# Max products on four banks with maxima taken in pairs, and scores on one pair of banks, in a fused decoder layer

## The chip, the core and the metric

The kernel runs on one core of a Trainium2 chip. The engines of the core, PE (TensorE, matrix products into PSUM), DVE (VectorE), ACT (ScalarE), POOL (GpSimd) and SP (SyncE, which issues most of the DMAs), each run an instruction stream of their own and meet at semaphores. PSUM is used as eight banks of 128 x 512 f32, `ps[:, 0]` to `ps[:, 7]`. The metric is the time of one execution in microseconds (us), the median of the runs.

## The reference, cut to what matters

One decoder layer on four batch rows of 512 tokens. Each batch runs through an attention with 16 heads of 32, a state-space model (a scan over 512 steps for 16 states) and a gated feed-forward, each followed by a layer norm. What the change touches is the softmax of the attention:

```python
q, k, v = heads(x @ Wq), heads(x @ Wk), heads(x @ Wv)
scores = jnp.einsum('bhqd,bhkd->bhqk', q, k) / jnp.sqrt(jnp.float32(D))
attn = jax.nn.softmax(scores, axis=-1)
std = jnp.einsum('bhqk,bhkd->bhqd', attn, v)
```

A softmax needs the maximum of each row of scores before it takes exponentials. Beside it stands a second attention by affinities to eight "splats" of each head, blended in with a small weight.

## The kernel before, in words

The batches run one behind the other. In a batch the attention is computed in four groups j = 0 to 3 of four heads each (`NG` = 4, `HG` = 4). The scores are computed twice.

First, as max products: for each group 16 tiles (four heads by four query tiles, numbered n = 16 j + i in the batch), a matmul each (`max_scores`, L1303) of 128 queries by 512 keys into bank 0 or 1 in turn. DVE takes the maximum over the keys (`max_tiles`, L960) into a column of `MX`. PE may start tile n when DVE has reduced tile n - 2 (`s_mx`). When all 16 are there, PE transposes the maxima (`transpose_max`, L1309), ACT negates them (`bias_row`, L642) and sends them by a DMA into a row of `QS`, from where the second scores get them as an additional row of the product.

Second, as transposed scores with the maximum subtracted: in the loop of `attention_phase` on PE, for each group four steps kt = 0 to 3 over the key tiles, and in each step two pairs of heads p = 0, 1 (L1413). ACT takes the exponential of a pair, two banks at once, into `PT` (L731, `s_exp`). The pairs stand in banks 2, 3 and 4, 5; a pair of scores waits for the exponential of the pair before the last. Only in group 3 of all but the last batch both pairs use banks 4 and 5, since banks 2 and 3 serve the preparation of the next batch there. Then `values` (L1320) multiplies the exponentials with V into bank 6, and with ones into bank 7 for the denominators; it runs one step behind the scores. The first call of a group into bank 6 waits until `normalise` of the group before has read banks 6 and 7 (`s_nrm`, L967).

Around this, while group j is in its score loop, the max products of group j + 1 are put between its matmuls, and DVE takes their maxima: `X_CHUNK` says how many of the 16 tiles in which step (for j = 0 tiles 4 to 8, 8 to 14, 14 to 16; for j = 1 and 2 tiles 0 to 4, 4 to 10, 10 to 16 in steps 0, 1 and 2), and `cuts` how many behind which pair. The first four tiles of group 1 (`X_AHEAD`) run before the loop.

Each engine works in the order of its program. On DVE a step of the loop is: the maxima, `normalise` of the group before (L966 to L970; for j = 2, `KV_GROUP`, ahead of the maxima, together with `splat_kv`, L1010, which needs the KV product of L1420), for j = 0 in step 1 the splat work (L979 to L993), and then halves of the state-space scan (`scan_half`: L896, the scan itself L904, L907). In batch 0 three or four halves fall to a group, one in step 1 and the others in step 3; in the other batches two, in step 3. On ACT a step is: decay exponentials for the scan (L593), in step 3 the bias row, and the two exponentials; at the turn to the next group `inverse_start` (a logarithm, L661, and an exponential, L663) stands ahead, for j = 1 a copy too (L712), and for j = 0 four splat exponentials follow step 0 (L649, L650).

## Time and profile before

| | us |
|---|---|
| median of three runs | 1462.55 |
| lowest, highest run | 1458.94, 1462.65 |
| the profiled execution | 1458.29 |
| its span, first to last instruction | 1456.5 |
| PE, DVE, ACT busy in it | 1211.8, 1204.7, 764.0 |

The profile is of one execution. A row of the timeline gives start, duration, engine, line of the kernel, operation, tiles, the number of instructions merged into it, and in brackets how long the engine was idle ahead of it and what ended that. PE overlaps its matmuls, so that the durations of neighbouring rows overlap; the distance of two starts says more. PEclk is the granted clock of PE: 1.00 is 2.4 GHz, 0.50 is 1.2 GHz.

### The profile page before, as it was taken

Reading aid. Unit: us, or ns where it says so; the run is one execution under the profiler, and the core shown is the slowest. Engines: PE = TensorE matmul, PEld = TensorE weight load, DVE = VectorE, ACT = ScalarE, POOL = GpSimd, SP = SyncE. Lnnn points to the kernel's source line nnn. Section 1 sums busy time; section 2 is a strip of 40 time slices with the busy share of each in tenths; the row PEclk is TensorE's granted clock in tenths of the full one; section 3 lists DMA queues with packets and bytes.
Section 4 is the critical chain, followed back from the end, with each engine's and each line's share of the span. In section 5 each row is a group of like instructions: output and inputs, shape, how many; then the busy total and the mean of one; then the engine's idle time right before and its main releaser. Section 6 shows DMA issues by size and latency. Waiting matters only on the chain.

```text
span 1456.5 us, 14224 instructions
## 1 busy us (share of the span) xinstructions
PE 1211.8 (83%) x4698; PEld 558.9 (38%) x4698; DVE 1204.7 (83%) x1457; ACT 764.0 (52%) x1118; POOL 164.9 (11%) x211
## 2 busy tenths in 40 slices
PE   5563885788689989889899898889799898877996
PEld 3332422233245543333345533333355433323553
DVE  5878898989979998879889997889799998786223
ACT  6865543535367753537477653545677545352331
POOL 1000111001101120100101121001111211001001
PEclk8765796878979999789899997899799997788998
DMA  6853796465339959553259686362289595540231
GB/s 193 288 162 116 172 255 165 102 145 145 58 89 248 251 133 266 127 132 87 67 135 272 164 225 194 90 164 51 89 230 259 119 256 133 146 95 15 66 101 44
DMA packets 112666, 220.20 MB, mean 151 GB/s; under 512 B 14560, under 2 KB 25312, under 8 KB 112592
## 3 DMA queue, kind: packets, MB, share of 16 engines
q1 hardware_dynamic: 88608, 142.85, 31.9%
q0 software_dynamic: 18432, 67.12, 23.9%
q10 hardware_dynamic: 5552, 9.31, 1.8%
q8 instruction: 38, 0.62, 0.2%
q14 instruction: 36, 0.29, 0.1%
HBM read 122.37 MB, written 29.62 MB: 104 GB/s over the span
## 4 chain that ended last, share of the span: by engine, by line
PE 38%; DVE 38%; issue 9%; ACT 4%; DVEq 0%; ACTq 0%; POOL 0%; POOLq 0%
DVE ST L904 14%; PE ps L1381 6%; DVE ST L896 5%; PE ps L1514 5%; PE ps L1303 5%; DVE MX L960 5%; PE ps L1320 4%; PE ps L1458 3%; PE ps L1378 3%; PE ps L1474 3%; PE ps L1413 2%; DVE QAK L1131 2%; DVE QS L1118 2%; DVE ST L907 1%; PE ps L1286 1%
## 5 line engine op out<-in xcount | busy, mean ns | idle before, releaser
L904 DVE TENSOR_TENSOR_SCAN ST<-dA,ST 128x1024 f32<-128x1024 f32 x128 | 292.9, 2289 | 12.9 <-ACT dA L593 10.2
L1514 PE MATMUL ps<-V,GU 128*128 128x512 f16 x1024 | 238.0, 387 | 5.6 <-DVE V L1105 5.6
L960 DVE TENSOR_REDUCE MX<-ps 128x1 f32<-128x512 f32 x256 | 165.2, 686 | 72.8 <-PE ps L1303 72.3
L509 POOL DMA_DIRECT2D YA<-ST x128 | 109.3, 854 | 975.6 <-DVE ST L907 923.8
L593 ACT ACTIVATE dA<-DL,Aneg 128x511 f32<-128x511 f32 x256 | 168.3, 713 | 60.6 <-DVE ST L904 56.4
L731 ACT ACTIVATE PT<-ps 128x1024 f32<-128x1024 f32 x128 | 126.8, 1021 | 135.7 <-PE ps L1413 135.0
L1303 PE MATMUL ps<-KS,QS 96*128 96x512 f32 x256 | 127.4, 562 | 50.1 <-DVE MX L960 37.1
L907 DVE TENSOR_TENSOR ST<-ST,BC 128x1024 f32<-128x1024 f32 x128 | 156.8, 1225 | 4.4
L896 DVE TENSOR_TENSOR ST<-DU,BC 128x1024 f32<-128x1024 f32 x128 | 155.9, 1218 | 0.1
L1514 PEld LDWEIGHTS ps<-V,GU 128*128 128x128 bf16 x1024 | 97.0, 99 | 140.6 <-issue 30.5
L1474 PE MATMUL ps<-QS 128*128 128x512 f32 x512 | 142.9, 422 | 2.5 <-DVE QS L1118 1.6
L1381 PE MATMUL ps<-XA,W 128*128 128x512 f32 x256 | 113.3, 595 | 0.0
L1303 PEld LDWEIGHTS ps<-KS,QS 96*128 96x128 f32 x256 | 56.5, 235 | 145.2 <-DVE MX L960 99.4
L1474 PEld LDWEIGHTS ps<-QS 128*128 128x128 f32 x512 | 97.6, 194 | 34.9 <-DVE QS L1118 11.3
L1413 PE MATMUL ps<-QS,KS 97*128 97x512 f32 x256 | 100.2, 490 | 6.6 <-ACT PT L731 5.6
L1131 DVE TENSOR_TENSOR QAK<-QAK,ps 128x512 f32<-128x512 f32 x64 | 43.7, 683 | 62.3 <-PE ps L1514 62.3
L1320 PE MATMUL ps<-PT,V 128*32 128x512 f32 x512 | 82.3, 720 | 12.4 <-ACT PT L731 9.9
L782 ACT CAST QS<-QAK 128x512 fp32r<-128x512 f32 x64 | 39.6, 618 | 95.2 <-DVE QAK L1131 95.2
L1320 PE MATMUL ps<-PT,ones 128*32 128x512 f32 x512 | 74.2, 654 | 0.0
L1413 PEld LDWEIGHTS ps<-QS,KS 97*128 97x128 f32 x256 | 52.0, 222 | 54.2 <-issue 27.7
L1381 PEld LDWEIGHTS ps<-XA,W 128*128 128x128 f32 x256 | 48.0, 190 | 62.6 <-issue 62.2
L1378 PE MATMUL ps<-W,XA 128*128 128x512 f32 x128 | 61.3, 639 | 4.2 <-ACT V L676 3.4
(231 smaller groups left out, 1539.9 us busy)
## 6 DMA issues: line engine op xcount, KB each, us to landing
YA<-ST POOLq DMA_DIRECT2D x128, 512.0 KB, 7.2
BC<-bc_rows SPq DMA_DIRECT2D x64, 512.0 KB, 8.0
GU<-gu_tiles SPq DMA_DIRECT2D x64, 256.0 KB, 4.6
QS<-proj_tiles SPq DMA_DIRECT2D x64, 256.0 KB, 4.2
QS<-qk_parts SPq DMA_DIRECT2D x32, 256.0 KB, 4.1
KS<-qk_parts SPq DMA_DIRECT2D x32, 256.0 KB, 5.5
ST<-in_L_ffn_w_gate_up_dram SPq DMA_DIRECT2D x16, 256.0 KB, 3.7
gu_tiles<-BC SPq DMA_DIRECT2D x16, 256.0 KB, 2.1
```

What stands on the lines that cost most here:

```text
L593: last = nc.scalar.activation(dA[:, a, e, 1:S], DL[:, 2 * a + e, 1:S], ACT.Exp, scale=Aneg[:, 2 * a + e, n:n + 1])
L731: nc.scalar.activation(PT[:, kt % 2, 2 * p:2 * p + 2, :], ps[:, bank:bank + 2, :], ACT.Exp, scale=SCALE).then_inc(s_exp, 1)
L896: nc.vector.tensor_tensor(ST[:, ring(bb, n, a), :, :], DU[:, 2 * a:2 * a + 2, :], BC[:, n % BC_RING, 0:1, :].broadcast_to((P, 2, S)), ALU. ...
L904: nc.vector.tensor_tensor_scan(flat, dA[:, a, :, :].rearrange("p e s -> p (e s)"), flat, 0.0, ALU.mult, ALU.add).then_inc(s_scan, 1)
L907: nc.vector.tensor_tensor(st, st, BC[:, n % BC_RING, 1:2, :].broadcast_to((P, 2, S)), ALU.mult).then_inc(s_prod, 1)
L960: nc.vector.tensor_reduce(MX[:, j % 2, qt, h:h + 1], ps[:, n % 2, :], AX_X, ALU.max).then_inc(s_mx, 1)
L1303: mm(ps[:, n % 2, :], QS[i][0:3 * D, h, qt * P:(qt + 1) * P], KS[i][0:3 * D, h, :], start=True, stop=True).then_inc(s_xs, 1)
L1320: last = mm(ps[D * h:D * h + D, bank, :], w, PT[:, kt % 2, h, :], start=(kt == 0), stop=(kt == KT - 1), tile_position=(0, D * h))
L1381: last = mm(bank, W[:, z, k, j * P:(j + 1) * P], XA[:, k, :], start=(k == 0), stop=(k == KT - 1))
L1413: last = mm(ps[:, score_bank(b, j, h), :], KS[i][0:3 * D + 1, h, kt * P:(kt + 1) * P], QS[i][0:3 * D + 1, h, :], start=True, stop=True)
L1474: last = mm(ps[:, 4 + r, :], HL[:, 2 * z + t % 2, r * P:(r + 1) * P], WP[:, t % WP_RING, :], start=(t == 0 and z == 0), stop=(t == NT - 1 ...
L1514: last = mm(ps[:, f % F_RING, :], GU[:, t % GU_RING, k, m * P:(m + 1) * P], XHL[:, z, k, :], start=(k == 0 and z == 0), stop=(k == KT - 1 ...
```

## The change

From tile n = 20 on (`FIRST_MAX_PAIR`: the 16 tiles of group 0 and the first four of group 1 stay as they are) the max products go to banks 0 to 3 in turn, and DVE takes the maxima of two tiles in one reduction over two banks. PE may start a pair when DVE has reduced the pair before the last. For this the scores give banks 2 and 3 away: in every group and batch both pairs of heads use banks 4 and 5, and a pair waits for the exponential of the pair just before it. In groups 0 to 2 the two `values` calls of a step move from behind both score pairs and their first max products to places between: bank 6 behind the first pair, bank 7 behind the second, each ahead of the max products of that place.

```diff
-        def score_bank(b, j, h):
-
-            return 4 + h % 2 if j == NG - 1 and b + 1 < B else 2 + h
+        def score_bank(h):
+
+            return 4 + h % 2
+
+        def max_bank(n):
+
+            return n % 2 if n < FIRST_MAX_PAIR else n % 4
...
+        FIRST_MAX_PAIR = 4 * KT + X_AHEAD
...
             def max_tiles(b, j, lo, hi):
-                for i in range(lo, hi):
+                pairs = 16 * j + lo >= FIRST_MAX_PAIR
+                for i in range(lo, hi, 2 if pairs else 1):
                     n = 16 * j + i
                     h, qt = i // KT, i % KT
-                    dve.wait_ge(s_xs, 16 * NG * b + n + 1)
-                    nc.vector.tensor_reduce(MX[:, j % 2, qt, h:h + 1], ps[:, n % 2, :], AX_X, ALU.max).then_inc(s_mx, 1)
+                    bank = max_bank(n)
+                    if pairs:
+                        dve.wait_ge(s_xs, 16 * NG * b + n + 2)
+                        nc.vector.tensor_reduce(MX[:, j % 2, qt:qt + 2, h], ps[:, bank:bank + 2, :], AX_X, ALU.max).then_inc(s_mx, 2)
...
-                    if n >= 2:
+                    if n >= FIRST_MAX_PAIR + 2:
+                        pe.wait_ge(s_mx, 16 * NG * b + n // 2 * 2 - 2)
+                    elif n >= FIRST_MAX_PAIR:
+                        pe.wait_ge(s_mx, 16 * NG * b + FIRST_MAX_PAIR)
+                    elif n >= 2:
                         pe.wait_ge(s_mx, 16 * NG * b + n - 1)
...
                             s = 2 * (KT * j + kt) + p
-                            if s < 2:
+                            if s == 0:
                                 pe.wait_ge(s_dist, 2 * (b + 1))
                                 pe.wait_ge(s_pj2, 2 * (b + 1))
                             else:
-                                one_pair = j == NG - 1 and not last_batch
-                                pe.wait_ge(s_exp, 2 * KT * NG * b + (s if one_pair else s - 1))
+                                pe.wait_ge(s_exp, 2 * KT * NG * b + s)
...
+                            if j < NG - 1 and kt > 0:
+                                values(b, j, kt - 1, 6 + p)
                             max_scores(b, j + 1, cuts[p], cuts[p + 1])
...
                         for p in range(2):
-                            if kt > 0 and j < NG - 1:
-                                values(b, j, kt - 1, 6 + p)
                             max_scores(b, j + 1, cuts[2 + p], cuts[3 + p])
```

## Rows read from the trace of the kernel before

**Rows 1.** The page, part 1: busy time, share and instructions of each engine.
```profile
PE 1211.8 (83%) x4698; PEld 558.9 (38%) x4698; DVE 1204.7 (83%) x1457; ACT 764.0 (52%) x1118; POOL 164.9 (11%) x211
```
**Rows 2.** The page, part 4: the chain that ended last, by engine.
```profile
PE 38%; DVE 38%; issue 9%; ACT 4%; DVEq 0%; ACTq 0%; POOL 0%; POOLq 0%
```
**Rows 3.** Waits, 880 to 985 us: us in total, times, longest us.
```profile
DVE MX L960 <- PE ps L1303: 19.9, 22, 2.4
...
PE ps L1303 <- DVE MX L960: 5.3, 7, 1.7
```
**Rows 4.** Stretches: us, busy time (instructions) of PE, PEld, DVE, ACT, POOL, PEclk, DMA.
```profile
902.00:912.00 10.00, 9.91 (x26) 5.35 (x26) 5.72 (x10) 6.31 (x8) 2.27 (x3) 0.50 0.28 54
...
930.00:936.00 6.00, 5.07 (x14) 1.84 (x15) 4.23 (x7) 1.61 (x2) 0.00 (x0) 0.50 0.71 169
...
937.00:957.00 20.00, 16.89 (x89) 6.48 (x81) 17.50 (x20) 9.98 (x13) 1.70 (x2) 1.00 0.50 116
```
**Rows 5.** The page, part 5: groups; busy us, mean ns of one, idle ahead.
```profile
L960 DVE TENSOR_REDUCE MX<-ps 128x1 f32<-128x512 f32 x256 | 165.2, 686 | 72.8 <-PE ps L1303 72.3
...
L896 DVE TENSOR_TENSOR ST<-DU,BC 128x1024 f32<-128x1024 f32 x128 | 155.9, 1218 | 0.1
...
L1131 DVE TENSOR_TENSOR QAK<-QAK,ps 128x512 f32<-128x512 f32 x64 | 43.7, 683 | 62.3 <-PE ps L1514 62.3
```
**Rows 6.** Timeline of batch 2, j = 0, end of kt 1: start us, us.
```profile
909.27 1.94 PE L1320 MATMUL ps<-PT,V 128*32 128x512 f32 x8
...
911.14 1.22 PE L1303 MATMUL ps<-KS,QS 96*128 96x512 f32 x2
...
913.18 0.87 DVE L979 TENSOR_SCALAR X<-X,par 128x512 f32<-128x512 f32 x2
...
916.59 1.28 DVE L960 TENSOR_REDUCE MX<-ps 128x1 f32<-128x512 f32 x2
```
**Rows 7.** Timeline of batch 2, j = 0 kt 3 and j = 1 kt 0.
```profile
919.98 1.94 ACT L731 ACTIVATE PT<-ps 128x1024 f32<-128x1024 f32 x2 [0.71 <-PE ps L1413]
...
921.97 1.06 PE L1320 MATMUL ps<-PT,V 128*32 128x512 f32 x8 [0.67 <-ACT PT L731]
...
924.24 1.18 PE L1413 MATMUL ps<-QS,KS 97*128 97x512 f32 x4
...
925.60 1.94 ACT L731 ACTIVATE PT<-ps 128x1024 f32<-128x1024 f32 x2
...
927.23 2.57 DVE L960 TENSOR_REDUCE MX<-ps 128x1 f32<-128x512 f32 x4
...
927.96 1.10 PE L1303 MATMUL ps<-KS,QS 96*128 96x512 f32 x2 [1.66 <-DVE MX L960]
```
**Rows 8.** Timeline of batch 2, j = 1, kt 0 to kt 2.
```profile
930.31 0.74 DVE L967 SCALAR_TENSOR_TENSOR X<-ps,par,RD 128x512 f32<-128x512 f32 x1
...
933.75 1.94 PE L1320 MATMUL ps<-PT,V 128*32 128x512 f32 x8
...
937.74 0.73 PE L1413 MATMUL ps<-QS,KS 97*128 97x512 f32 x2
...
938.31 0.63 PE L1303 MATMUL ps<-KS,QS 96*128 96x512 f32 x2
...
942.05 1.29 DVE L960 TENSOR_REDUCE MX<-ps 128x1 f32<-128x512 f32 x2 [0.73 <-PE ps L1303]
```
**Rows 9.** Timeline of batch 2, j = 2, kt 0: the KV product and splat_kv.
```profile
950.24 3.60 PE L1420 MATMUL ps<-V,QAK 128*128 128x512 f32 x8
...
954.68 0.74 DVE L1010 SCALAR_TENSOR_TENSOR QAK<-ps,par,head_mask 128x512 f32<-128x512 f32 x1
```
**Rows 10.** Timeline of batch 0: j = 0 kt 1, and maxima of j = 1.
```profile
254.90 1.91 ACT L731 ACTIVATE PT<-ps 128x1024 f32<-128x1024 f32 x2
...
256.58 0.88 DVE L979 TENSOR_SCALAR X<-X,par 128x512 f32<-128x512 f32 x2
...
295.37 1.29 DVE L960 TENSOR_REDUCE MX<-ps 128x1 f32<-128x512 f32 x2 [1.90 <-PE ps L1303]
```

More of the change, by code:

```diff
@@ L729, in attention_phase @@
                                     act.wait_ge(parts, 64 * (b + 1))
-                            bank = score_bank(b, j, 2 * p)
+                            bank = score_bank(2 * p)
                             nc.scalar.activation(PT[:, kt % 2, 2 * p:2 * p + 2, :], ps[:, bank:bank + 2, :],
@@ L955, in max_tiles @@
             def max_tiles(b, j, lo, hi):
-                for i in range(lo, hi):
+                pairs = 16 * j + lo >= FIRST_MAX_PAIR
+                for i in range(lo, hi, 2 if pairs else 1):
                     n = 16 * j + i
                     h, qt = i // KT, i % KT
-                    dve.wait_ge(s_xs, 16 * NG * b + n + 1)
-                    nc.vector.tensor_reduce(MX[:, j % 2, qt, h:h + 1], ps[:, n % 2, :], AX_X, ALU.max).then_inc(s_mx, 1)
+                    bank = max_bank(n)
+                    if pairs:
+                        dve.wait_ge(s_xs, 16 * NG * b + n + 2)
+                        nc.vector.tensor_reduce(MX[:, j % 2, qt:qt + 2, h], ps[:, bank:bank + 2, :], AX_X, ALU.max).then_inc(s_mx, 2)
+                    else:
+                        dve.wait_ge(s_xs, 16 * NG * b + n + 1)
+                        nc.vector.tensor_reduce(MX[:, j % 2, qt, h:h + 1], ps[:, bank, :], AX_X, ALU.max).then_inc(s_mx, 1)
             def normalise(b, j):
@@ L1302, in max_scores @@
                         pe.wait_ge(s_ka, b + 1)
-                    mm(ps[:, n % 2, :], QS[i][0:3 * D, h, qt * P:(qt + 1) * P], KS[i][0:3 * D, h, :],
+                    mm(ps[:, max_bank(n), :], QS[i][0:3 * D, h, qt * P:(qt + 1) * P], KS[i][0:3 * D, h, :],
                        start=True, stop=True).then_inc(s_xs, 1)
@@ L1412, in attention_phase @@
                             for h in (2 * p, 2 * p + 1):
-                                last = mm(ps[:, score_bank(b, j, h), :], KS[i][0:3 * D + 1, h, kt * P:(kt + 1) * P],
+                                last = mm(ps[:, score_bank(h), :], KS[i][0:3 * D + 1, h, kt * P:(kt + 1) * P],
                                           QS[i][0:3 * D + 1, h, :], start=True, stop=True)
```

## The prediction

> **What bounds the kernel now.** The page first: PE and DVE are each busy 83% of the span, ACT 52% [rows 1], and the chain that ended last runs 38% over PE and 38% over DVE [rows 2]. No engine bounds the whole; the work passes from one to the other, so the change has to be priced where it acts: in groups j = 0, 1 and 2 of the attention loop of each batch. I read batch 2 (902 to 980 us) as the pattern of batches 1 to 3, and batch 0 by itself, because it has a scan half ahead of the last maxima of a group.
>
> In that stretch PE waits for a maximum of DVE only seven times, 5.3 us in all, at most 1.7 us; DVE waits for the products 22 times, 19.9 us [rows 3]. So two banks for the max products cost PE little. The products come late to DVE because PE has other work, and has it at the lower clock: 902 to 912 and 930 to 936 us show a granted clock of 0.50, which is 1.2 GHz, with PE 85 to 99% busy; 937 to 957 us shows 1.00, which is 2.4 GHz [rows 4]. The end of a group (kt 3) and the turn to the next are DVE's: two halves of the scan fill it from the last maximum, 917.9 us [rows 6], to the next, 927.23 [rows 7], while PE has less to do.
>
> **Part 1: maxima by pairs.** From tile 20 on, 44 single reductions of a batch become 22 of 1024 elements. A single takes 686 ns [rows 5], and four in a row take 2.57 us, 0.64 each [rows 7]. The pair's form is not in the trace. TENSOR_TENSOR costs 683 ns for 512 and 1218 ns for 1024 elements [rows 5], 535 ns for the second half, so I take 686 + 535 = 1.22 us. Bounds: 0.97 us, what ACT takes for two banks (two in 1.94 us [rows 7]), and 1.37, two singles. In a row a pair saves 0.11 us, 2.4 us a batch, 9.7 in all, if DVE never waited. Against it stands a latency: a pair starts when both products are there and is through 1.22 us behind the second, where a single came 0.7 behind it.
>
> **Part 2: four banks.** PE may run a pair ahead while DVE reduces another. What that gives is at most the 5.3 us a batch of waits [rows 3]; the largest is the gap of 1.66 us at 926.3, where PE waits for the end of the scan [rows 7].
>
> The Trainium skill, "TensorE: Matmul & The Clock Gate", section on HAM oscillation, reports a matmul kernel in which PSUM double-buffering gave no further gain. The row of 1.66 us speaks for some gain here; by the page the maxima of batch 0, below, would win nothing back and the sum would be 3 us higher.
>
> **Part 3: scores on one pair of banks.** Each score pair now waits for the exponentials of the pair just before it, about 1.0 us on ACT, not of the one before that. In steps 1 and 2 of a group the values that now stand between (1.0 us at 2.4 GHz [rows 7], 1.87 at 1.2 [rows 6]) and two max products cover it. At two places nothing does.
> Step kt 3: ACT has the bias row and its DMA issue ahead, so its two exponentials start at 919.98 and PE goes on with values at 921.97 [rows 7]. Afterwards the second scores start at 921.05 and their exponential ends at 922.7: +0.75 us for PE.
> Step kt 0 of j = 1 and 2: nothing stands between the score pairs, and ACT has logarithm and inverse ahead (for j = 1 a copy too), so the first exponential starts at 925.60 [rows 7]. The second scores start at 926.65 instead of 924.8: +1.85. Queued behind them on PE are the first four max products, for j = 2 behind the 3.6 us of the KV product.
>
> **Part 4: values moved ahead.** values(kt 0, bank 6) now stands right behind the first scores of kt 1, ahead of the max products and of the second scores. It waits for s_nrm, the second operation of normalise(j - 1). For j = 2 DVE does that first, for j = 1 only after four maxima. Before, that call began at 933.75, long after normalise (930.31 plus 0.74) [rows 8].
>
> **The groups, added up (batch 2).**
> j = 0. values(bank 7) now runs ahead of the last four max products of kt 1, where it stood behind them, and the second scores of kt 0 and kt 1 wait for ACT some 0.5 us: by the same order of steps the products end at 913.5 instead of 912.4 [rows 6]. Two pairs behind each other end at 915.5; DVE was through at 913.2. Its splat work (913.18 to 916.59) and the last pair follow: 920.1 instead of 917.9, +2.3 us. No scan covers this, since the transposes of the maxima stand ahead of kt 3 on PE.
> j = 1. Without that shift the first two products end at 928.6 (kt 3 and kt 0 above, less what PE was ahead); DVE asks for them at 927.23 [rows 7]: +1.35. Two pairs take until 931.0, normalise frees values at 932.3, and two products follow at 934 to 935. Then PE has no waits: at 2.4 GHz 0.57 us for a score pair, 0.5 for a product pair [rows 8], so 4.0 from those values to the end of kt 1, 4.6 for kt 2, and 1.2 for the last pair: 942.1, where the last maximum now ends at 943.34 [rows 8]; 1.2 early. With 1.2 GHz through kt 1 (1.87 for values, 0.85 for each pair) it is 3.1 us later, 1.9 late. I take +1.4, nearer the low clock, because PE's gap ahead of it is longer than now.
> j = 2. KV product and splat_kv come 0.75 + 1.85 us later, less 0.85 that the KV product had in hand (950.24 plus 3.60 is 953.84, splat_kv starts at 954.68 [rows 9]): +1.75. The four products behind it save about 0.95 of waits, the last pair costs 0.3: +1.1. With the clock high through kt 1 it would be 3.6 less, 2.5 early.
> Together 2.3 + 1.4 + 1.1 = 4.8 us a batch, 14.4 for batches 1 to 3. Group j = 3 follows with DVE late from its start, so nothing is won back.
> Batch 0. In j = 0 the first exponential of kt 1 runs at 254.90, behind splat and decay exponentials [rows 10]. The second scores now wait for its end, 255.95; with them, one values and four products PE is through at 258.5, two pairs end at 260.5, where DVE had its six maxima at 256.58 [rows 10]: +3.9. In j = 1 and 2 the turn costs 2.6 each as above, but the last six maxima stand behind a scan half, and there four banks pay: the idle 1.90 us between them [rows 10] and most of the pairs' gain come back. I take +1.0 and +0.2: 5.1 us, with 1 and 10 as bounds.
> Last batch, j = 3, which now waits as the other batches' did: three steps of 0 to 0.75 us each, +1.
>
> Sum 14.4 + 5.1 + 1.0 = 20.5 us. The profiled execution took 1458.3 us (span 1456.5), 4.3 below the median 1462.55 and just below the fastest of the three runs; on its own time the sum is 1479, on the median 1483.
>
> **Rivals.**
> A, PE slower still. The gap of 1.66 us at 926.3 [rows 7] was followed by the low clock from 930 [rows 4]. The change makes new gaps: 2.9 us ahead of kt 3 of j = 0 (values done at 917.2, transposes at 920.1), 1.85 at both turns, 2.4 ahead of values in j = 1. If the clock falls there already, kt 3 or the KV product runs at 1.2 GHz: four values at 0.9 more, less the 0.75 that they then cover, some 3 us a turn, two turns in three batches: +18, 1501. The Trainium skill's page named above, section on the second failure mode, tells of short gaps between matmul groups that cycle through PSUM banks and keep the clock oscillating.
> B, faster. It decides on whether the clock stays at 2.4 GHz at the turns to j = 1 and 2, because four products run at once there and the wait for DVE's scan is gone. Then a batch costs 2.3 - 1.2 - 2.5 = -1.4, and batch 0 some -2 by its maxima behind a scan: -6, 1456. Against it: PE's gap moves to the exponential; it does not go.
> C, no difference. The turns hide under DVE's 9.3 us of scan, and only j = 0 is paid: 3 x 2.3 + 3.9 = 10.8, less the 9.7 of the pairs: +1, 1464.
> D, the pair doesn't save what it says: 1.37 us each. 88 times 0.15 on a chain that is partly PE's there: up to +9 more, 1492.
>
> **How the numbers follow.** Forecast 0.50, A 0.15, B 0.12, C 0.15, D 0.08. The time is the forecast's, 1483; its own range, 1469 to 1496, is from the clock bounds of j = 1 and 2 and those of batch 0. The range given reaches from C's lower edge, 1460, into A, 1503. About 0.3%, 4.4 us, is what a measurement of this kernel can tell from no change: faster 0.12 (B), same 0.15 (C), slower 0.73.
>
> **What would show it.** In the profile after: pair reductions of 1.2 us; values of kt 0 in j = 1 waiting for normalise's second operation; the second scores of kt 0 waiting for ACT near 1.9 us in j = 1 and 2; in j = 0 DVE's splat operations two microseconds later against the first scores; the granted clock at the turns. I am wrong if the first maximum of j = 1 does not come later behind the scan, or if the low stretches of the clock shorten.

## The result, and the profile after

The changed kernel takes 1503.4 us in the median (1497.21 to 1505.45, four runs) where the kernel before took 1462.2 beside it: the ratio is 1.0284, 95% interval 1.0255 to 1.0313, 41 us slower. The side was forecast; the size, 20.5 us, was half of what came. The profiled execution of after took 1505.45 us with a span of 1503.7, 47.2 longer than the span of before.

The page of after, parts 1, 4 and 5 (busy time; chain; groups with busy us, mean ns of one, idle ahead):

```profile
PE 1221.1 (81%) x4693; PEld 556.9 (37%) x4698; DVE 1197.8 (80%) x1369; ACT 768.7 (51%) x1118; POOL 164.9 (11%) x211
...
PE 39%; DVE 30%; issue 9%; ACT 6%; DMA 3%; SPq 1%; DVEq 0%; ACTq 0%; POOL 0%; POOLq 0%
...
L968 DVE TENSOR_REDUCE MX<-ps 128x2 f32<-128x1024 f32 x88 | 105.1, 1222 | 82.9 <-PE ps L1318 82.9
```

Against [rows 1] DVE has 7 us less to do and PE 9 more; both lose share, since they wait. Against [rows 2] the chain passes 8% less over DVE, and DMA and SP, which were not in the chain before, hold 4% of it: a transfer has become late. A pair takes 1.222 us, the value assumed.

To see where the time lies, take from the timeline of PE the start of the transposes of each group (L1309 before, L1324 after; of batch 2, 917.92 and 944.31 for those that end j = 0). Their distances are the lengths of the groups. Summed over the four batches (j = 0 starts here at the transposes of group 0), with the time at 1.2 GHz beside them, which is 2 x (1 - granted clock) x length, over eight equal stretches of each group:

| us | j = 0 | j = 1 | j = 2 | at 1.2 GHz in the three |
|---|---|---|---|---|
| before | 87.6 | 110.2 | 114.8 | 130 |
| after | 102.9 | 127.8 | 119.8 | 157 |
| longer by | 15.3 | 17.6 | 5.0 | 27 |
| forecast | 10.8 | 5.2 | 3.5 | |

The rest, 9.3 of the 47.2 us, lies in group 3 (some 6, where the forecast had 1.0) and outside the attention. Of the three groups j = 1 is the one that is far off. Its turn in batch 2, timeline of after (start, us, engine, line, in brackets the idle time ahead):

```profile
944.31 0.60 PE L1324 MATMUL ps<-ident,MX 128*4 128x128 f32 x4 [3.02 <-DVE MX L968]
...
947.32 0.73 PE L1427 MATMUL ps<-QS,KS 97*128 97x512 f32 x2 [0.95 <-ACT PT L736]
...
953.87 0.73 PE L1427 MATMUL ps<-QS,KS 97*128 97x512 f32 x2 [1.73 <-ACT PT L736]
...
956.73 2.08 PE L1318 MATMUL ps<-KS,QS 96*128 96x512 f32 x4 [2.13 <-DMA KS<-qk_parts]
...
958.06 2.36 DVE L968 TENSOR_REDUCE MX<-ps 128x2 f32<-128x1024 f32 x2 [4.37 <-PE ps L1318]
...
960.93 0.74 DVE L978 SCALAR_TENSOR_TENSOR X<-ps,par,RD 128x512 f32<-128x512 f32 x1
...
961.82 1.94 PE L1335 MATMUL ps<-PT,V 128*32 128x512 f32 x8 [2.16 <-DVE X L978]
...
965.01 1.23 DVE L968 TENSOR_REDUCE MX<-ps 128x2 f32<-128x1024 f32 x1 [2.61 <-PE ps L1318]
```

Three waits stand behind each other on PE at one turn: 1.73 us for the exponential, 2.13 for a DMA, 2.16 for `normalise`. The first and the last were in the forecast. The one between was not. The granted clock behind them (us, busy PE, PEld, DVE, ACT, POOL, PEclk, DMA):

```profile
956.00:962.00 6.00, 3.11 (x10) 2.03 (x14) 3.90 (x5) 1.02 (x1) 0.00 (x0) 0.52 1.06 248
962.00:968.00 6.00, 6.00 (x24) 2.22 (x20) 1.75 (x3) 1.02 (x1) 0.00 (x0) 0.63 0.09 33
```

PE does the two steps that should win the time back at 1.2 GHz for most of 12 us. The DMA is the reload of `QS` and `KS` for group j + 2, which SP starts when the last scores of kt 3 are done (`s_s`). The queue of SP, the store of `YA` that POOL issues and the first max products, first of before, then of after:

```profile
919.48 0.59 SPq L381 DMA_DIRECT2D QS<-qk_parts  x1
...
921.54 0.59 SPq L383 DMA_DIRECT2D KS<-qk_parts  x1
...
922.89 0.85 POOL L509 DMA_DIRECT2D YA<-ST  x1 [18.61 <-DVE ST L907]
...
925.25 0.39 PE L1303 MATMUL ps<-KS,QS 96*128 96x512 f32 x1
```

```profile
948.09 0.59 SPq L386 DMA_DIRECT2D QS<-qk_parts  x1
...
949.27 0.86 POOL L514 DMA_DIRECT2D YA<-ST  x1 [21.36 <-DVE ST L912]
...
949.97 0.59 SPq L388 DMA_DIRECT2D KS<-qk_parts  x1
```

Against the transposes, SP starts 1.56 us behind them before (919.48 - 917.92) and 3.78 after (948.09 - 944.31). The fourth of the eight DMAs, the last that the first max products of group 2 need, is issued at 949.97 and they start at 956.73, 6.76 us later. Before, they start 3.71 us behind it (925.25 - 921.54) and wait for no DMA. So the later start, 2.2 us, is not all: the data also take at least 3 us longer. In after the store of `YA`, 512 KB, is issued ahead of the fourth DMA, before it came behind; e6 below comes back to that.

### The profile page after: what moved, and what is told of

Its sections match the earlier page's. It is cut to its first block, busy times and chain, and to the rows that moved or that the text cites. A ratio compares the mean times of both kernels' runs of the same rounds, so it can differ in the third digit from the quotient of the medians.

```text
span 1503.7 us, 14219 instructions
## 1 busy us (share of the span) xinstructions
PE 1221.1 (81%) x4693; PEld 556.9 (37%) x4698; DVE 1197.8 (80%) x1369; ACT 768.7 (51%) x1118; POOL 164.9 (11%) x211
## 4 chain that ended last, share of the span: by engine, by line
PE 39%; DVE 30%; issue 9%; ACT 6%; DMA 3%; SPq 1%; DVEq 0%; ACTq 0%; POOL 0%; POOLq 0%
DVE ST L909 11%; PE ps L1396 6%; PE ps L1335 6%; PE ps L1528 5%; DVE ST L901 4%; PE ps L1318 4%; PE ps L1427 4%; PE ps L1472 3%; PE ps L1393 3%; DVE MX L968 2%; PE ps L1488 2%; ACT PT L736 2%; DVE QAK L1142 2%; DVE QS L1129 2%; DMA YA<-ST 1%
## 5 line engine op out<-in xcount | busy, mean ns | idle before, releaser
L909 DVE TENSOR_TENSOR_SCAN ST<-dA,ST 128x1024 f32<-128x1024 f32 x128 | 293.0, 2289 | 12.1 <-ACT dA L598 9.4
L736 ACT ACTIVATE PT<-ps 128x1024 f32<-128x1024 f32 x128 | 130.9, 1022 | 165.0 <-PE ps L1427 158.6
L968 DVE TENSOR_REDUCE MX<-ps 128x2 f32<-128x1024 f32 x88 | 105.1, 1222 | 82.9 <-PE ps L1318 82.9
L1318 PE MATMUL ps<-KS,QS 96*128 96x512 f32 x256 | 109.6, 525 | 40.9 <-DVE MX L971 20.0
L1427 PE MATMUL ps<-QS,KS 97*128 97x512 f32 x256 | 109.7, 516 | 36.6 <-ACT PT L736 35.4
L1318 PEld LDWEIGHTS ps<-KS,QS 96*128 96x128 f32 x256 | 51.5, 226 | 131.0 <-DVE MX L971 43.9
L1335 PE MATMUL ps<-PT,V 128*32 128x512 f32 x512 | 85.5, 746 | 9.6 <-DVE X L978 8.6
L1427 PEld LDWEIGHTS ps<-QS,KS 97*128 97x128 f32 x256 | 51.6, 229 | 95.6 <-ACT PT L736 75.1
L1335 PE MATMUL ps<-PT,ones 128*32 128x512 f32 x512 | 78.7, 691 | 0.0
L971 DVE TENSOR_REDUCE MX<-ps 128x1 f32<-128x512 f32 x80 | 51.4, 685 | 19.7 <-PE ps L1318 19.7
```

Source lines behind the costliest of these rows:

```text
L736: nc.scalar.activation(PT[:, kt % 2, 2 * p:2 * p + 2, :], ps[:, bank:bank + 2, :], ACT.Exp, scale=SCALE).then_inc(s_exp, 1)
L909: nc.vector.tensor_tensor_scan(flat, dA[:, a, :, :].rearrange("p e s -> p (e s)"), flat, 0.0, ALU.mult, ALU.add).then_inc(s_scan, 1)
L968: nc.vector.tensor_reduce(MX[:, j % 2, qt:qt + 2, h], ps[:, bank:bank + 2, :], AX_X, ALU.max).then_inc(s_mx, 2)
L1318: mm(ps[:, max_bank(n), :], QS[i][0:3 * D, h, qt * P:(qt + 1) * P], KS[i][0:3 * D, h, :], start=True, stop=True).then_inc(s_xs, 1)
L1335: last = mm(ps[D * h:D * h + D, bank, :], w, PT[:, kt % 2, h, :], start=(kt == 0), stop=(kt == KT - 1), tile_position=(0, D * h))
L1427: last = mm(ps[:, score_bank(h), :], KS[i][0:3 * D + 1, h, kt * P:(kt + 1) * P], QS[i][0:3 * D + 1, h, :], start=True, stop=True)
```

## The experiments

Lengths of the groups as above, longer or shorter than the 87.6, 110.2 and 114.8 of before, with the medians' difference from the kernel before, run beside each (us).

The lengths are of one profiled execution of each kernel. How far they repeat can be seen in j = 0 of batch 0, where e9, e10 and e13 to e17 have the instructions of before: it takes 26.7 us in before and in e17, 28.3 to 28.6 in the six others. So +1 to +2 in the column j = 0 is no effect of the edit in their rows. And e6 was profiled in its slowest run, 1490.63 us.

| | time | j = 0 | j = 1 | j = 2 | at 1.2 GHz |
|---|---|---|---|---|---|
| scores on one pair alone (e2) | +48.7 | +14.4 | +18.5 | +11.1 | 159 |
| after, values put back (e1) | +28.1 | +15.9 | +5.8 | +3.4 | 136 |
| values between, alone (e6) | +22.1 | +6.0 | +12.9 | +1.2 | 116 |
| after, single maxima (e3) | +35.7 | +11.7 | +15.9 | 0.0 | 128 |
| wait at the turn alone (e9) | +12.3 | +1.0 | +6.2 | +2.0 | 137 |
| wait in kt 3 alone (e10) | +31.0 | +1.9 | +18.9 | +5.9 | 166 |
| the same, early reload (e14) | +25.2 | +1.6 | +5.5 | +5.3 | 137 |
| after, early reload (e4) | +38.4 | +13.0 | +8.2 | +10.4 | 148 |
| after, normalise first (e5) | +27.1 | +15.3 | +4.3 | +3.1 | 136 |
| after, dummy products (e7) | +31.7 | +14.5 | +14.2 | -2.4 | 121 |
| after, all three (e11) | +14.5 | +13.9 | -7.8 | +0.4 | 111 |
| all three, j = 0 as before (e13) | -14.0 | +1.8 | -14.6 | -2.6 | 74 |
| that, no dummy products (e16) | -10.6 | +1.9 | -13.3 | +2.7 | 98 |
| e13, single maxima (e17) | -19.8 | 0.0 | -15.9 | -3.7 | 69 |
| before, early reload and normalise first (e15) | -2.4 | +1.9 | -0.6 | +0.4 | 134 |
| before, dummy products in group 0 (e8) | -1.2 | -3.0 | +2.5 | -0.1 | 108 |
| the same in batches 1 to 3 (e12) | -1.2 | -5.4 | -1.5 | -0.1 | 97 |

**The parts one by one.** The first kernel is after with `values` behind both score pairs again; the second is before with the scores on banks 4 and 5 and nothing else.

```diff
# e1, against after
-                            if j < NG - 1 and kt > 0:
-                                values(b, j, kt - 1, 6 + p)
...
+                            if kt > 0 and j < NG - 1:
+                                values(b, j, kt - 1, 6 + p)
# e2, against before
-            return 4 + h % 2 if j == NG - 1 and b + 1 < B else 2 + h
+            return 4 + h % 2
...
-                            if s < 2:
+                            if s == 0:
...
-                                one_pair = j == NG - 1 and not last_batch
-                                pe.wait_ge(s_exp, 2 * KT * NG * b + (s if one_pair else s - 1))
+                                pe.wait_ge(s_exp, 2 * KT * NG * b + s)
```

> The changed kernel with the two values calls of a step back behind both score pairs and their first max products; four banks, pairs and the one pair of score banks stay. Theory (the loss is a sum of new PE waits: exponentials at kt 3 and kt 0, values ahead of the products, the reload of QS and KS): the values' wait for normalise in j = 1 (2.2 us a batch) and the late products of j = 0 (some 1.5 us) go, but score pairs of kt 1 to 3 now wait for the exponential uncovered, 0.2 to 0.8 us each; net 5 to 15 us faster than the changed kernel, 1488 to 1498. Rival 1 (the order of values is the main cause): within 10 us of the kernel before, under 1473. Rival 2 (the latency of the pairs is the main cause): no difference from the changed kernel, 1500 to 1506.

> The kernel before with one edit: all scores on banks 4 and 5, each pair waiting for the exponential of the pair just before. Max products stay on two banks with single maxima, values stay where they were. Theory: this alone costs most of the loss, 1.85 us at the turns, 0.75 and more in kt 3, and the reload of QS and KS that starts behind the second scores of kt 3: 20 to 35 us over the kernel before, 1482 to 1497. Rival 2 (pairs' latency): within 5 us of the kernel before. Rival 1 (order of values): within 10 us of the kernel before.

Measured: e1 1488.66 us, 1.0198 [1.0163, 1.0233]; e2 1509.24, 1.0329 [1.0296, 1.0363]. One score pair alone costs more than the whole change, and more than the 20 to 35 us expected of it; e1 came out within its forecast. Four banks and pairs then give 20.6 us back (e2 to e1), and moving the values costs 15 again (e1 to after). PE's waits for the exponential in e2 (engine, total us, times, longest):

```profile
PEld ps L1412 <- ACT PT L731: 113.1, 69, 6.2
```

These are the weight loads of the scores. Before, they waited 18.2 us for it; in after 75.1, where the values stand between, and 112.0 in e1, where they do not. So the values do cover part of the wait, as the forecast had it, but standing between the scores they make j = 1 longer: 17.6 there in after, 5.8 in e1.

**The values and the maxima alone.** e6 is before with `values` moved between the score pairs; e3 is after with single maxima, a tile waiting for the one four before it.

```diff
# e6, against before
+                            if j < NG - 1 and kt > 0:
+                                values(b, j, kt - 1, 6 + p)
...
-                            if kt > 0 and j < NG - 1:
-                                values(b, j, kt - 1, 6 + p)
# e3, against after
-                pairs = 16 * j + lo >= FIRST_MAX_PAIR
+                pairs = False
...
-                        pe.wait_ge(s_mx, 16 * NG * b + n // 2 * 2 - 2)
-                    elif n >= FIRST_MAX_PAIR:
-                        pe.wait_ge(s_mx, 16 * NG * b + FIRST_MAX_PAIR)
+                        pe.wait_ge(s_mx, 16 * NG * b + n - 3)
```

> The kernel before with one edit: the values calls of groups 0 to 2 between the score pairs, as changed; two banks with single maxima, scores on two pairs of banks. It prices the order of values without the waits for exponentials. Theory: products come later to DVE in kt 1 and 2, and in j = 1 values wait for normalise: 8 to 20 us over the kernel before, 1470 to 1482. If the order costs only together with the one pair of score banks: within 4 us of the kernel before.

> The changed kernel with single maxima from tile 20 on (PE waits for tile n - 4), four banks, scores and values as changed. Theory: pairs save 0.11 us in a row where DVE is late and cost about 0.5 us of latency where PE is late, and PE is late in most places: within 6 us of the changed kernel, 1497 to 1506. Rival 2 (latency of the pairs is the cause): 10 to 25 us faster than the changed kernel. The gain of the pairs as meant: some 5 to 10 us slower.

Measured: e6 1482.56, 1.0152 [1.0108, 1.0197], at the edge of its forecast; 12.9 of its groups' 20.1 us are in j = 1. By batches j = 1 is longer there by 4.8, 1.0, 6.3 and 0.9 us. The values wait 1.28 us for `normalise` in all four, so that is not what makes the difference between them. PE waits 5.06 and 4.17 us for KS in batches 0 and 2, and 0.67 and 0.92 in 1 and 3: here too the values stand ahead of the second scores of kt 3, and the reload starts later. Batch 1, then batch 2 (the fourth DMA, the store of `YA`, the first max products):

```profile
622.67 0.59 SPq L383 DMA_DIRECT2D KS<-qk_parts  x1
622.99 0.86 POOL L509 DMA_DIRECT2D YA<-ST  x1 [19.10 <-DVE ST L907]
...
626.17 0.73 PE L1303 MATMUL ps<-KS,QS 96*128 96x512 f32 x2 [0.67 <-DMA KS<-qk_parts]
```

```profile
942.96 0.85 POOL L509 DMA_DIRECT2D YA<-ST  x1 [19.87 <-DVE ST L907]
...
943.77 0.60 SPq L383 DMA_DIRECT2D KS<-qk_parts  x1
...
950.67 1.22 PE L1303 MATMUL ps<-KS,QS 96*128 96x512 f32 x2 [4.17 <-DMA KS<-qk_parts]
```

Issued ahead of the store, the data are there 3.50 us later; issued 0.81 us behind it, 6.90 us later. In the profiles of after, e2, e3, e5, e6, e7 and e10, PE waits for KS at the turn to j = 1 in 21 places: in the 19 where the fourth DMA is issued behind the store its data come 6.5 to 7.7 us after the issue, in the two where it is issued ahead of it (e6) 3.5 and 3.8. A reload that starts two microseconds later thus comes behind the store and loses some three more. No run moves the store alone, so that it is the reason stays an inference from this order.

e3 1496.22, 1.0232 [1.0178, 1.0286], just below its forecast: without the pairs the median is lower, but the intervals of e3 and after overlap, so a gain without the pairs is not shown, nor one with them.

**The two places where a score pair newly waits.** Each is before with the one wait added: e9 at the turn to j = 1 and 2, e10 in kt 3 of j = 0 to 2. e14 is e10 with the reload of heads 0 and 1 started after the first scores of kt 3.

```diff
# e9, against before
+                                one_pair = one_pair or (j in (1, 2) and kt == 0 and p == 1)
# e10, against before
+                                one_pair = one_pair or (j < NG - 1 and kt == KT - 1 and p == 1)
# e14, against e10
-                    sp.wait_ge(s_s, 2 * KT * NG * b + 2 * KT * (j - 1))
+                    sp.wait_ge(s_s, 2 * KT * NG * b + 2 * KT * (j - 1) - 1)
...
+                    if j >= 2 and pair == 1:
+                        sp.wait_ge(s_s, 2 * KT * NG * b + 2 * KT * (j - 1))
```

> The kernel before with one additional wait: in kt 0 of j = 1 and 2 the second scores wait for the exponential of the first. Nothing else changes (banks, order, maxima as before). It measures the term 'turn' of the forecast by itself: 1.35 us in j = 1 and about 1.0 to 1.75 in j = 2, 9 to 13 us in all, 1469 to 1474. If the turn was the term that was mis-sized (the clock falls by the new gap): 20 us or more, over 1480. If it hides under DVE's scan: within 4 us of before.

> The kernel before with one additional wait: in kt 3 of j = 0, 1 and 2 the second scores wait for the exponential of the first. With the values behind both score pairs this costs PE some 2.1 us a group, and the reload of QS and KS starts 2.1 us later. Forecast's view (it hides partly under 9.3 us of scan): 1.0 us in j = 1, 1.3 in j = 2, some in j = 3, 8 to 14 us in all, 1468 to 1475. If the late reload and the clock come on top: 18 us or more, over 1478. If it is all hidden: within 4 us of before.

> The kernel before with the wait of kt 3 (second scores wait for the first exponential, j = 0 to 2), and with the reload of QS and KS for heads 0, 1 started after the first scores of kt 3 instead of the last. Theory (most of the 31 us of that wait is the late reload, seen as waits of PE for KS of 3.2, 3.4 and 3.9 us at the turns to j = 1, and the low clock behind them): 1472 to 1480. Rival (the wait itself and the clock make it, the reload was ready anyway by the time DVE asked): 1487 to 1491.

Measured: e9 1472.33, 1.008 [1.0066, 1.0095]; e10 1490.98, 1.0208 [1.0193, 1.0224]; e14 1483.38, 1.0169 [1.0154, 1.0185]. The turn costs what was expected, 12 us. The wait in kt 3, added to the kernel before, costs 31; there the values stand behind both score pairs, so that PE idles 2.18 us where the forecast had 0.75 for the changed order. In the timeline of e10 in batch 2, the second scores of kt 3, the first max products of j = 1 and the first maximum:

```profile
941.22 0.73 PE L1414 MATMUL ps<-QS,KS 97*128 97x512 f32 x2 [2.18 <-ACT PT L731]
...
950.95 1.23 PE L1303 MATMUL ps<-KS,QS 96*128 96x512 f32 x2 [3.92 <-DMA KS<-qk_parts]
...
951.78 1.29 DVE L960 TENSOR_REDUCE MX<-ps 128x1 f32<-128x512 f32 x2 [4.43 <-PE ps L1303]
```

Such waits for KS stand in three of the four batches (3.17, 3.43 and 3.92 us); PE has none before. In e14 they are gone, and most of the lengthening of j = 1 with them: +5.5 instead of +18.9. But the time falls by 5.8 us only, so neither expectation of e14 held. In its profile the rest, outside the three groups, is 13 us longer than before's where e10's was 7. Of these 6 us, 3.8 lie ahead of the first group (its transposes stand at 242.13 us in e14, at 238.35 in e10), where the two kernels do the same work: they are the spread of single executions. Group 3 is 7 us longer than before's in e10 and 9 in e14. Of the 31 us, then, the late reload is 6 by the medians and 14 by the lengths of the three groups. The rest belongs to the wait itself with what it does to the clock and to group 3; how it divides was not measured.

**Three mends in the changed kernel.** e4 starts the reload early (the diff of e14, on after). e5 puts `normalise` ahead of the maxima in j = 1 too. e7 fills PE's wait at the turn with two products into a bank that nobody reads.

```diff
# e5, against after
-                        if j == KV_GROUP and c == 0:
+                        if j in (1, KV_GROUP) and c == 0:
                             normalise(b, j - 1)
+                        if j == KV_GROUP and c == 0:
                             splat_kv(b)
...
-                        if j > 0 and j != KV_GROUP and c == 0:
+                        if j == NG - 1 and c == 0:
# e7, against after, behind the scores
+                            if j in (1, 2) and kt == 0 and p == 0:
+                                for _ in range(2):
+                                    mm(ps[:, 3, :], ident[:, :], W[:, 3, 0, :], start=True, stop=True)
# e11: the edits of e4, e5 and e7 on after
```

> The changed kernel, but the reload of QS and KS for group j + 2 starts for heads 0 and 1 when the first scores of kt 3 are through (they are the last readers of these heads), and only heads 2 and 3 wait for the second scores. Theory: PE's wait for that transfer at the turn to j = 1 (1.97, 2.13 and 1.94 us in three of the batches of the profiled run) goes, and with it the clock falls less: 5 to 9 us faster than the changed kernel, 1494 to 1498. Rival: the transfer is late because the DMA queues are full, not because it starts late: no difference, 1500 to 1506.

> The changed kernel, but DVE does normalise of group 0 ahead of the first four maxima of j = 1, as it does for j = 2 anyway. DVE idles there 4.2 to 4.4 us for the products, so that normalise fits in. Theory (values ahead of the products wait for normalise behind four maxima): PE's wait of 2.16 us for it goes in all four batches, and DVE's own 2 us of normalise leave the path: 8 to 16 us faster than the changed kernel, 1487 to 1495. Rival: values' wait is cover for the pairs that DVE still has to reduce, so that PE only waits later: within 4 us of the changed kernel.

> The changed kernel with two additional products of a constant into the free bank 3 between the two score pairs of kt 0 in j = 1 and 2, where PE waits 1.7 us for the exponential; their result is overwritten. Only PE's gap changes. Theory that the gaps bring the clock down: the low stretch behind the turns is shorter or gone, 1.5 to 3 us at each of eight turns where the granted clock now falls, 6 to 15 us faster than the changed kernel, 1488 to 1497. Rival: the waits themselves are the loss and the clock falls by the other gaps as well: within 4 us of the changed kernel.

> The changed kernel with the three mends together: early reload for heads 0 and 1, normalise ahead of the maxima in j = 1, and PE's gap at the turn filled. By themselves they gave 4, 14 and 10 us. Theory that they take away three different waits: 20 to 28 us faster than the changed kernel, 1473 to 1482, and what is left over the kernel before is the forecast's j = 0, kt 3 and turn. If they share one cause (the clock at the turn): no better than the best of them, 1485 to 1490.

Measured: e4 1498.98, 1.0256 [1.0229, 1.0283]; e5 1487.61, 1.019 [1.0165, 1.0214]; e7 1492.21, 1.0216 [1.0171, 1.0262]; e11 1474.5, 1.0087 [1.0071, 1.0104]. Against after's +41.2 they save 2.8, 14.1 and 9.5 us, 26.4 in all, and 26.7 together, so that by the medians the prices add up. The interval of e4 overlaps that of after by half, so that its 2.8 us are not shown; that of e7 still touches it, those of e5 and e11 lie clear of it. In e5 j = 1 takes 13.3 us less than in after; DVE does `normalise` first and the values no longer wait for it, though the late DMA is still there (batch 2):

```profile
944.91 0.74 DVE L978 SCALAR_TENSOR_TENSOR X<-ps,par,RD 128x512 f32<-128x512 f32 x1
...
948.50 2.08 PE L1319 MATMUL ps<-KS,QS 96*128 96x512 f32 x4 [2.04 <-DMA KS<-qk_parts]
...
951.35 1.94 PE L1336 MATMUL ps<-PT,V 128*32 128x512 f32 x8
```

The early reload alone takes 9.4 us from j = 1 and gives 5.4 of them back in j = 2, where batches 1 to 3 have 10 us each at 1.2 GHz. Batch 2 of e4, with the transposes at 936.96:

```profile
947.83 2.36 DVE L970 TENSOR_REDUCE MX<-ps 128x2 f32<-128x1024 f32 x2 [1.49 <-PE ps L1320]
...
951.59 1.94 PE L1337 MATMUL ps<-PT,V 128*32 128x512 f32 x8 [2.38 <-DVE X L980]
```

The values start 14.63 us after the transposes, though they still wait for `normalise`; in after 17.51.

**The clock by itself.** e8 is before with dummy products into bank 6 at the end of the max products of group 0, and with a wait (`s_hi`) ahead of them; e12 does so in batches 1 to 3 only.

```diff
-                max_scores(b, 0, 12, 16)
+                def warm(columns):
+                    mm(ps[:, 6, 0:columns], ident[:, :], W[:, 3, 0, 0:columns], start=True, stop=True)
+
+                pe.wait_ge(s_hi, 2 * NG * (b + 1))
+                max_scores(b, 0, 12, 14)
+                warm(S // 2)
+                max_scores(b, 0, 14, 16)
+                warm(S)
                 transpose_max(b, 0)
+                warm(S)
```

> The kernel before with additional products of a constant into the free bank 6 at the end of group 0's max products (one of 256 columns, two of 512, about 2 us of PE work a batch, in places where PE waits 0.4 to 0.8 us for DVE or ACT); the result is overwritten. Theory that the low clock of 902 to 912 us comes from PE's gaps ahead of it: the granted clock of that stretch is 1.00 in batches 1 to 3 and the kernel is 5 to 10 us faster than before, 1450 to 1456. Rival: the clock falls anyway, and the products cost up to 1 us a batch: 1460 to 1466.

> The kernel before with the additional products of e8 in batches 1 to 3 only, since batch 0 lost 5 us with them in the profiled run. Theory: 3 to 6 us faster than before, 1454 to 1458. Rival (the clock falls a few us later instead and the gain is given back): within 2 us of before.

Measured: e8 1459.32, 0.999 [0.9974, 1.0006]; e12 1458.84, 0.9993 [0.9976, 1.001]. No difference, although the clock did rise. The stretch of 583 to 600 us, ahead of j = 0 of batch 1, before and in e8:

```profile
583.00:600.00 17.00, 14.72 (x44) 7.09 (x44) 10.89 (x19) 9.31 (x13) 3.29 (x3) 0.60 0.43 111
```

```profile
583.00:600.00 17.00, 14.70 (x47) 5.97 (x47) 13.71 (x22) 7.33 (x12) 3.31 (x3) 1.00 0.70 208
```

By the groups j = 0 of batch 1 falls from 20.3 to 17.3 us in e8 (19.9 and 19.4 in batches 2 and 3), but batch 0 is some 4 us longer there than in before's profile. In e12 batches 2 and 3 show the same 17.3, and some 3.5 us are lost ahead of the groups. So the low clock of j = 0 does cost up to 3 us a batch, in the kernel before too; dummies put ahead of it cost about as much, and what is left is below what these runs can tell from nothing. Time at 1.2 GHz is no measure of the loss by itself: the three groups have 108 and 97 us of it here, 130 before.

**A version that beats both.** After the three mends almost all that is left is j = 0 (+13.9). e13 is e11 with j = 0 as before: scores on banks 2 to 5, values behind, single maxima on two banks for all of group 1; in the last batch j = 3 uses both pairs too. e16 is e13 without the dummy products, e17 is e13 (dummies included) with single maxima, e15 is before with the early reload and `normalise` first alone.

```diff
# e13, against e11
+        def both_pairs(b, j):
+            return j == 0 or (j == NG - 1 and b + 1 == B)
-            return 4 + h % 2
+            return 2 + h if both_pairs(b, j) else 4 + h % 2
...
-        FIRST_MAX_PAIR = 4 * KT + X_AHEAD
+        FIRST_MAX_PAIR = 8 * KT
...
-                                pe.wait_ge(s_exp, 2 * KT * NG * b + s)
+                                pe.wait_ge(s_exp, 2 * KT * NG * b + (s - 1 if both_pairs(b, j) else s))
...
-                            if j < NG - 1 and kt > 0:
+                            if 0 < j < NG - 1 and kt > 0:
                                 values(b, j, kt - 1, 6 + p)
...
+                            if j == 0 and kt > 0:
+                                values(b, j, kt - 1, 6 + p)
# e16, against e13: the three lines of e7 left out
# e17, against e13: the edit of e3
# e15, against before: the edits of e14 (SP) and e5 (DVE)
```

> The changed kernel with its three mends (reload of heads 0, 1 earlier, normalise ahead of the maxima in j = 1, two dummy products at the turn), and with group j = 0 put back: scores on banks 2 to 5, values behind both score pairs, single maxima on banks 0 and 1 for all of group 1; the last batch's j = 3 has both pairs of banks again too. The row sums of the profile with the three mends show 6.5, 3.0, 1.9 and 2.9 us gained in j = 0 of the four batches, 14.3 of its 16.7. Theory (what is left of the loss is j = 0 alone, by the scores on one pair of banks): 1460, 1455 to 1464, no slower than the kernel before, and what four banks and pairs give behind a scan in batch 0 (-3 us) may show as a gain. Rival (the loss of j = 0 comes back in j = 1, where the products then have to be ready at the same time and meet the same normalise): 1466 to 1474.

> The kernel before, with two of the mends alone: normalise ahead of the maxima in j = 1, and the reload of QS and KS for heads 0, 1 after the first scores of kt 3. No four banks, no pairs, no change of the scores. Theory (the gain of group 0 as before plus mends comes from the four banks and pairs, and normalise was late for nobody in the kernel before): 0.998 to 1.004 of the kernel before. Rival (the gain of 13 us was the mends' own, normalise and reload were late in the kernel before too): 0.991 to 0.994.

> The fastest version (group 0 as before, the three mends) without the two dummy products at the turns to j = 1 and 2. Theory (they hold the clock at the turns, 11 us in the changed kernel): 1452 to 1457. Rival (with the maxima of group 1 back on two banks, PE comes to the turn with more in hand, and the products cover nothing that anyone waits for): 1442 to 1447.

> The fastest version with single maxima on the four banks (a tile waits for the one four before it): the pairs are taken away, 32 in a batch become 32 + 32 singles. Theory (the pairs save 0.11 us of DVE each but hold the last product's maximum back, as the changed kernel with singles showed, 1.0232 against 1.0284): 1440 to 1444, no slower. Rival (DVE sets the pace in j = 1 and 2 behind the normalise, and 64 singles cost 0.11 x 32 a batch there): up to 14 us more, 1450 to 1458.

Measured: e13 1444.24, 0.9901 [0.9885, 0.9918]; e15 1458.78, 0.9978 [0.9959, 0.9997]; e16 1450.51, 0.9936 [0.9908, 0.9965]; e17 1441.35, 0.9859 [0.9822, 0.9895]. Against their forecasts: e13 is below both of its ranges, e16 between its two, e15 at the edge of the one without a gain, e17 within the one that has the pairs do nothing. Putting j = 0 back gains twice what its own lengthening was: besides the 12.1 us of j = 0, j = 1 gains 6.8 and j = 2 3.0, and the rest is outside the three. The whole of group j = 1 of batch 2, from transposes to transposes, before, after and in e13:

```profile
917.92:943.40 25.48, 21.49 (x105) 8.39 (x106) 21.39 (x26) 13.25 (x18) 1.70 (x2) 0.87 0.50 125
```

```profile
944.31:974.99 30.68, 21.53 (x105) 8.71 (x106) 20.77 (x18) 12.82 (x16) 1.70 (x2) 0.83 0.44 104
```

```profile
911.98:934.60 22.62, 19.47 (x108) 8.27 (x109) 20.59 (x18) 13.15 (x17) 1.70 (x2) 1.00 0.56 141
```

PE does the same products, and the dummies, in 22.62 us instead of 25.48, at the full clock from end to end. At the turn of e13 no DMA is waited for, and `normalise` is through before the maxima:

```profile
918.73 1.88 PE L1438 MATMUL ps<-W,ident 128*128 128x512 f32 x4
...
921.19 1.09 PE L1324 MATMUL ps<-KS,QS 96*128 96x512 f32 x4
921.28 0.68 DVE L982 TENSOR_TENSOR X<-ps,RD 128x512 f32<-128x512 f32 x1
...
923.27 3.48 DVE L973 TENSOR_REDUCE MX<-ps 128x2 f32<-128x1024 f32 x3
```

Two mends alone (e15) are worth 2 us. The dummies are 3 to 6 of the gain by the medians (e16 against e13), but the intervals overlap a little and e16's ten runs spread from 1448.3 to 1463.2; j = 1 of its batches 1 and 2 takes 22.6 us at the full clock without any dummies. The pairs give nothing: with singles the median is lower again, as in e3, with overlapping intervals. The cleanest comparison for the banks is e16 with e15, both with the two mends and no dummies: 0.9936 against 0.9978. So four banks for the maxima of groups 2 and 3, with what they need of the scores and values there, are worth some 6 to 8 us once the turn is mended, though these intervals touch too. After and e1 have four banks without mends and are slower, but they have j = 0 changed as well; four banks with j = 0 as before and no mends was not run, and the dummies were not tried in the kernel before by themselves at the turn.

## Why the prediction was right and wrong

**Right.** The side and its reason: one pair of banks for the scores costs more than four banks and pairs give (e2, e1). The pair's 1.22 us. The wait at the turn: 1.73 us of idle time where 1.85 was worked out, and 12.3 us of time (e9), where its terms were put at 9 to 13 for that run. j = 0 of batches 1 to 3: 2.7, 2.8 and 3.2 us longer in after (23.0, 23.1 and 23.5 against 20.3), forecast 2.3. The idle time ahead of kt 3 of j = 0: 3.02 us, forecast 2.9. The order of events at the turn to j = 1, and its times where the reload is not late and the clock holds in kt 3 (below).

**Luck.** j = 2, 5.0 us where 3.5 was forecast: by batches it is -0.5, +2.9, -0.4 and +2.9. The two long ones have 10 us at 1.2 GHz, batch 2 has none. The forecast's 1.1 for batches 1 to 3 is none of these; it comes near their mean.

**Wrong: the term of j = 1**, 5.2 us in the four batches, which measured 17.6. The step that failed is "Without that shift the first two products end at 928.6": it carried kt 3's 0.75 and the turn's 1.85 us to PE's own next matmuls and left out SP, whose reload of QS and KS waits for those same scores; it also took kt 3 to stay at 2.4 GHz. Counted from the transposes, in batch 2: second scores of kt 0 at 8.73 us in the forecast (926.65 - 917.92), at 9.56 in after (953.87 - 944.31); both pairs through at 13.1 (931.0) and at 16.1 (958.06 + 2.36); values at 14.4 (932.3) and at 17.5 (961.82). Of these 3 us, 2.1 are the wait for KS and 0.8 the later scores. In batch 1 PE waits for no KS, and yet the values start at 17.85: kt 3 runs at 1.2 GHz there, the second scores of kt 0 come at 11.82, and by then the reload has landed. In batches 1 and 2 of e4 neither happens, and the forecast comes out: the first maxima start at 10.87 in batch 2 (forecast 928.6 - 917.92, 10.7), the values at 14.63 in both (14.4), and j = 1 is 1.0 and 2.1 us longer than before (1.4). So the order of events was right; the late reload, or the low clock in its stead, set everything three microseconds further on.

And then "at 2.4 GHz 0.57 us for a score pair": by the granted clocks of 0.52 and 0.63 PE did most of that work at half speed, which the text had as the bound of 1.9 us late, not as its value. j = 1 is longer by 3.4, 4.2, 5.2 and 4.8 us by batches, beyond that bound in each. e5 takes the wait for `normalise` away and keeps the late reload; 4.3 us of the 17.6 remain. e4 does the opposite, and 8.2 remain. So either mend alone takes most of the excess out of j = 1, and how the 17.6 divide between the two waits is not shown. By the time of the whole kernel the wait for `normalise` is the larger: 14.1 us saved (e5) against 2.8, not clear of the spread (e4), since e4 loses again in j = 2.

**Half right: kt 3**, "+0.75 us for PE". On PE it is right: the second scores start 3.01 us after the transposes in batch 2 of after (947.32 - 944.31), 3.13 in the forecast (921.05 - 917.92), with 0.95 us of idle time. What the term left out is what those scores release: the reload starts 2.2 us later. The 31 us of e10 are not this term, since there the values stand behind (2.18 us of idle time); they show how much a wait at this place can cost.

**Wrong: group 3**, put at +1 for the last batch alone and measured at some 6 over the four; no run looks into it by itself.

**Open: j = 0 of batch 0**, +3.9, which measured 6.6 in the two profiles (33.3 against 26.7), with 26.4 us at 1.2 GHz instead of 13.0. But the same instructions take 28.3 to 28.6 us with 18 to 22 at 1.2 GHz in e9, e10 and e13 to e16, and those of after 31.4 with 21 in e4. So the change costs 3 to 7 us there, and the forecast lies within; it had no term for the clock in batch 0. The products come late to DVE, which idles twice over three microseconds ahead of its splat work; one of the two:

```profile
257.75 1.23 DVE L968 TENSOR_REDUCE MX<-ps 128x2 f32<-128x1024 f32 x1 [3.27 <-PE ps L1318]
...
264.59 0.87 DVE L990 TENSOR_SCALAR X<-X,par 128x512 f32<-128x512 f32 x2
```

The splat work begins at 264.59 where it stood at 256.58 [rows 10], 1.4 of that from a later start of the batch.

**The rivals.** A, the clock lower still, gave 1501, the nearest time, and its cause is there in part: 27 us more at 1.2 GHz in the three groups, 13 of them in j = 0 of batch 0, where the same instructions spread by 9 from one profile to another. Where it was placed is borne out in batch 1, kt 3 of j = 0, by this stretch of after, which was at 1.00 before:

```profile
620.12:628.12 8.00, 7.41 (x36) 2.15 (x40) 7.90 (x5) 2.64 (x3) 0.86 (x1) 0.60 0.30 72
```

In batch 2 the same stretch (944.31 to 952.31) stayed at 1.00, and A knew nothing of the reload and gave `normalise` only the forecast's price. B asked for a clock that holds at the turns; after does not have it, e13 does, and e13 is faster. C fell with e9 and e10: the turns do not hide under the scan. D fell with 1222 ns; but that pairs save nothing is what e3 and e17 suggest. The latency named in part 1 would explain it; no run shows it by itself.

The Trainium skill, "TensorE: Matmul & The Clock Gate", section on HAM oscillation, has PSUM double-buffering without further gain in its kernel. Here four banks and pairs give 20.6 us from e2 to e1: the measurement differs, and decides. Its section on the second failure mode, short gaps between groups of matmuls that keep the clock swinging, agrees with the 130 to 157 us above and with the 0.52 and 0.63 behind the three waits.

## What to carry to other kernels

When an instruction starts later, follow every semaphore that it sends, not only the engine's own next work: here the scores also released a reload on SP, which no row of before showed as late because it never was; and ask what the later transfer then meets on the DMA engines. When several waits come to stand one behind the other at a turn, mend them one by one and together, and look at the clock of the stretch behind them: in batch 2 of after PE was granted 0.52 and 0.63 there. Read lengths of a few microseconds off a single execution only where another execution of the same instructions repeats them. And give a scarce buffer away only in those groups where what it releases is not on the path: with j = 0 left as it was and the turn mended, the kernel gained 10 to 20 us (e16, e13, e17), of which 2 are the mends' own (e15); with j = 0 changed too it lost 14 (e11).

## What was not expected of the hardware

Two products that compute nothing, put into a wait of PE at each turn, saved 9.5 us by the medians (e7), with 121 us at 1.2 GHz in the three groups instead of 157. The same kind of products, put at the end of the max products of group 0, raised the clock there as well (0.60 to 1.00 over 17 us) and won nothing (e8, e12). One reduction over two banks, 1222 ns against 685 for one bank and 1.18 against 0.64 each when they run back to back, saves 0.1 us for two tiles, and no gain of it shows in the time (e3, e17). And the reload of `QS` and `KS` came 3.5 to 3.8 us after its fourth issue when that went out ahead of the store of `YA`, and 6.5 to 7.7 us when it went out behind it.
